# Quantised cross attention in a decoder kernel: the turning of the probabilities moved from TensorE to DMA, and their rounding from VectorE to GpSimd

## What is computed

```python
q = (x @ Wq + bq).reshape(1, B * N, H, hd)            # H = 16 heads of hd = 16
kv = (cond @ Wkv + bkv).reshape(1, -1, 2, H, hd)
k, v = (kv[:, :, 0], kv[:, :, 1])
q = jnp.transpose(q * scale, (0, 2, 1, 3))            # k and v likewise, without the scale
q = _fq_sym(q, axis=-1); k = _fq_sym(k, axis=-1); v = _fq_sym(v, axis=2)
attn = jnp.einsum('bhqd,bhkd->bhqk', q, k)
attn = jax.nn.softmax(attn.astype(jnp.float32), axis=-1)
attn = _fq_unsigned(attn, axis=-1)                    # s = max/255; round(attn/s), 0 to 255, times s
out = jnp.einsum('bhqk,bhkd->bhqd', attn, v)
```

## Time and profile before

| what | value |
|---|---|
| median of three runs | 2290.28 us |
| the profiled execution's own time | 2290.69 us |
| its span | 2288.9 us |
| TensorE busy | 1893.1 us, 83% |
| VectorE busy | 1271.6 us, 56% |
| ScalarE busy | 806.8 us, 35% |
| GpSimd busy | 253.6 us, 11% |
| first score product to last row written, attention block | 1034.72 to 1331.25 us |

### The profile page before, as it was taken

One profiled execution on the slowest core, in us unless ns is written; L12 is line 12 of the kernel. 1 busy time (PEld: TensorE's weight loads), 2 busy tenths in 40 slices (PEclk: granted clock), 3 DMA queues, 4 the chain that ended last, 5 costly groups with the idle time before them and its releaser, 6 DMA issues. The chain is left out here.

```text
span 2288.9 us, 25404 instructions
## 1 busy us (share of the span) xinstructions
PE 1893.1 (83%) x8989; PEld 1106.2 (48%) x8990; DVE 1271.6 (56%) x2123; ACT 806.8 (35%) x1349; POOL 253.6 (11%) x256
## 2 busy tenths in 40 slices
PE   6899599844646666748999979989977999999998
PEld 4566246532312222435555553355645565555555
DVE  3457522467459999679999954434643222222224
ACT  2257211135354333127888832215621111111111
POOL 0100202021003322320000011110050000000000
PEclk9999799977778889875555579997997999999999
DMA  1100000110000000100000000000001323223220
GB/s 73 60 1 2 19 0 22 48 42 1 26 0 1 0 0 0 56 11 1 1 1 1 2 28 0 0 0 1 2 11 55 111 82 95 87 89 89 87 80 19
DMA packets 25002, 68.93 MB, mean 30 GB/s; under 512 B 3456, under 2 KB 10880, under 8 KB 23488
## 3 DMA queue, kind: packets, MB, share of 16 engines
q1 hardware_dynamic: 24896, 67.55, 9.3%
HBM read 66.23 MB, written 1.31 MB: 30 GB/s over the span
## 5 line engine op out<-in xcount | busy, mean ns | idle before, releaser
L2317 PE MATMUL psum<-XT,l3f_wgu 128*128 128x512 f32 x768 | 337.4, 592 | 0.0
L2359 DVE TENSOR_TENSOR l3f_h<-l3f_silu,psum 128x512 f32<-128x512 f32 x96 | 66.0, 688 | 363.1 <-ACT l3f_silu L2343 363.1
L2317 PEld LDWEIGHTS psum<-XT,l3f_wgu 128*128 128x128 f32 x768 | 145.9, 190 | 163.8 <-issue 161.3
L1581 PE MATMUL psum<-l_drive,consts 128*128 128x512 f32 x256 | 148.5, 710 | 92.3 <-DVE l_drive L1679 92.3
L2343 ACT ACTIVATE l3f_silu<-psum 128x512 f32<-128x512 f32 x96 | 57.3, 597 | 430.6 <-PE psum L2317 430.6
L2308 PE MATMUL psum<-l3f_wd,l3f_h 128*128 128x256 f32 x784 | 177.0, 379 | 0.0
L1903 ACT ACTIVATE l2x_rings<-psum,l2x_mx,l2x_q_s 128x1024 f32<-128x1024 f32 x128 | 154.2, 1205 | 47.1 <-DVE l2x_mx L1861 45.8
L2308 PEld LDWEIGHTS psum<-l3f_wd,l3f_h 128*128 128x128 f32 x784 | 149.0, 190 | 40.7 <-issue 23.0
L424 POOL TENSOR_TENSOR rstd<-var,minus_half 128x1 f32<-128x1 f32 x104 | 66.2, 637 | 914.0 <-DVE var L395 914.0
L1859 DVE TENSOR_REDUCE l2x_mx<-psum 128x1 f32<-128x1024 f32 x128 | 156.0, 1218 | 9.8 <-PE psum L1826 8.1
L1836 PEld LDWEIGHTS psum<-l2x_id,l2x_rings 128*128 128x128 f16 x1024 | 98.8, 141 | 126.0 <-DVE l2x_rings L1869 126.0
(11 more groups left out here) (439 smaller groups left out, 3099.9 us busy)
## 6 DMA issues: line engine op xcount, KB each, us to landing
l3f_wgu<-in_expert_gu SPq DMA_DIRECT2D x48, 256.0 KB, 2.6
l3f_c_all<-token_weights SPq DMA_DIRECT2D x32, 384.0 KB, 4.2
l3f_c_all<-token_weights SPq DMA_DIRECT2D x32, 256.0 KB, 4.3
l3f_wd<-in_expert_down SPq DMA_DIRECT2D x48, 128.0 KB, 2.4
l3f_c_all<-token_weights SPq DMA_DIRECT2D x32, 128.0 KB, 4.2
arena<-in_pack SPq DMA_DIRECT2D x1, 3660.0 KB, 11.9
arena<-in_pack SPq DMA_DIRECT2D x1, 3277.0 KB, 10.4
arena<-in_pack SPq DMA_DIRECT2D x1, 2688.0 KB, 9.9
```

Source lines behind the costliest of these rows:

```text
L1581: last = nc.tensor.matmul(k.bank(4 + 2 * e + half), k.identity[:, :], drive[:, (2 * i + e) % 4, half * HALF:(half + 1) * HALF], start=n == ...
L2317: last = nc.tensor.matmul(k.bank(2 * half + n), wgu[:, slot, c, n * P:(n + 1) * P], k.XT[:, c, half * HALF:(half + 1) * HALF], start=c == ...
```

## The change

- The scores have three pairs of banks (0 to 5), so that unit i waits for the exponential of unit i - 3. TensorE's transposes, their float16 identity and the copies out of PSUM are gone.
- The bias of the exponential has ln 255 added, in the instruction that scales the maximum. So the exponential and its sum are 255 times as large, the multiplication in the rounding and the 1/255 at the end of a tile fall away.
- GpSimd rounds: one instruction on 128 x 1024 float32 adds 1.5 * 2^23 and takes it away again, and writes bfloat16 into the ring `whole` of 3.
- SyncE issues for each unit one DMA with transpose=True, from `whole` into `pT`, now a ring of 4 with a semaphore for each slot. 256 KB a unit.
- The values come five units behind the scores in place of four.

```diff
-        rings = k.sb(ctx, "l2x_rings", [P, 6 * T])
+        rings = k.sb(ctx, "l2x_rings", [P, 13 * T // 2])
-        e16 = rings[:, 3 * T:9 * T // 2].bitcast(F16).rearrange("p (n t) -> p n t", n=3)
-        pT = rings[:, 9 * T // 2:].bitcast(BF16).rearrange("p (n c t) -> p n c t", n=3, c=TILES)
+        whole = rings[:, 3 * T:9 * T // 2].bitcast(BF16).rearrange("p (n t) -> p n t", n=3)
+        pT = rings[:, 9 * T // 2:13 * T // 2].bitcast(BF16).rearrange("p (n c t) -> p n c t", n=4, c=TILES)
...
-                nc.vector.tensor_copy(f16_id[:, :], k.identity[:, :])
...
+        units, lag = TILES * heads, 5
+        turned_into = [k.sem(f"l2x_turned_into{slot_}") for slot_ in range(4)]
+        score_banks = lambda u: k.psum[:, 2 * (u % 3):2 * (u % 3) + 2, :]
             @block.tensor
-                        if i >= 2:
-                            pe.wait_ge(exp, i - 1)
+                        if i >= 3:
+                            pe.wait_ge(exp, i - 2)
...
-                    if 2 <= i < units + 2:
-                        u = i - 2
-                        pe.wait_ge(rounded, u + 1)
...
-                            last = nc.tensor.transpose(k.bank(4 + u % 2).bitcast(F16)[:, c * P:(c + 1) * P],
-                                                       e16[:, u % 3, c * P:(c + 1) * P], f16_id[:, :])
-                    if i >= 4:
-                        u = i - 4
+                    if i >= lag:
+                        u = i - lag
+                        pe.wait_ge(turned_into[u % 4], 16 * (u // 4 + 1))
...
             @block.vector
-                        k.link(dve, "dve_step", nc.vector.tensor_reduce(
-                            mx[:, i % 4, 0:1], k.psum[:, 2 * (i % 2):2 * (i % 2) + 2, :], AX.XY, ALU.max, negate=True))
-                        nc.vector.tensor_scalar(mx[:, i % 4, 1:2], mx[:, i % 4, 0:1], q_s[:, i:i + 1], None,
-                                                ALU.mult).then_inc(max_, 1)
+                        nc.vector.tensor_reduce(mx[:, i % 4, 0:1], score_banks(i), AX.XY, ALU.max,
+                                                negate=True).then_inc(max_taken, 1)
...
+                        dve.wait_ge(max_taken, i + 1)
+                        nc.vector.tensor_scalar(mx[:, i % 4, 1:2], mx[:, i % 4, 0:1], q_s[:, i:i + 1], LOG_255,
+                                                ALU.mult, ALU.add).then_inc(bias_ready, 1)
-                        nc.vector.tensor_scalar(e16[:, u % 3, :], e[:, u % 3, :], 255.0, 1024.0,
-                                                ALU.mult, ALU.add).then_inc(rounded, 1)
...
-                        nc.vector.tensor_scalar(pT[:, u % 3, :, :], k.bank(4 + u % 2).bitcast(F16)
...
-                        k.link(dve, "dve_step", nc.vector.tensor_scalar(k.recip[:, :], k.recip[:, :], 1.0 / 255, None,
-                                                                        ALU.mult))
...
             @block.scalar
+                    act.wait_ge(bias_ready, i + 1)
+                    if i >= 3:
+                        act.wait_ge(rounded, i - 2)
...
-                        nc.scalar.activation(pT[:, u % 3, :, :], k.bank(4 + u % 2).bitcast(F16)
-                                             .rearrange("p (c t) -> p c t", c=TILES), ACT.Copy,
-                                             bias=-1024.0).then_inc(by_act, 1)
+            @block.gpsimd
+            def _(pool):
+                for i in range(units):
+                    pool.wait_ge(exp, i + 1)
+                    if i >= 3:
+                        pool.wait_ge(turned_into[(i - 3) % 4], 16 * ((i - 3) // 4 + 1))
+                    nc.gpsimd.tensor_scalar(whole[:, i % 3, :], e[:, i % 3, :], ROUND, -ROUND,
+                                            ALU.add, ALU.add).then_inc(rounded, 1)
+            @block.sync
+            def _(sp):
+                for i in range(units):
+                    sp.wait_ge(rounded, i + 1)
+                    if i >= 4:
+                        sp.wait_ge(added, i - 3)
+                    sp.dma_start(pT[:, i % 4, :, :], whole[:, i % 3, :], transpose=True).then_inc(turned_into[i % 4], 16)
```

More of the change, by code:

```diff
@@ L8 @@
 from contextlib import ExitStack
+import math
 import numpy as np
@@ L30 @@
 ROUND = 1.5 * 2.0 ** 23
+LOG_255 = math.log(255.0)
 STAGES = range(0, 12)
@@ L1716, in l2_xattn @@
     bq, bk, bv, bp = (w(n) for n in ("bq", "bk", "bv", "bp"))
-    F16 = mybir.dt.float16
     with ExitStack() as ctx:
@@ L1808, in l2_xattn @@
         project(k, "l2x_turn_kv", heads // 2 + 2, turn_kv, turn_kv_out)
[L1811 to L1815, removed]
+        units, lag = TILES * heads, 5
+        names = ("scores", "max_taken", "bias_ready", "exp", "rounded", "added", "row")
+        scores, max_taken, bias_ready, exp, rounded, added, row_done = (k.sem("l2x_" + n) for n in names)
+        turned_into = [k.sem(f"l2x_turned_into{slot_}") for slot_ in range(4)]
+        score_banks = lambda u: k.psum[:, 2 * (u % 3):2 * (u % 3) + 2, :]
         with nc.Block("l2x_attention") as block:
@@ L1818, in _ @@
             def _(pe):
-                for i in range(units + 4):
+                for i in range(units + lag):
                     if i < units:
@@ L1822, in _ @@
                         rows = slice(h % 2 * slot, h % 2 * slot + 3 * hd)
-                        if i >= 2:
-                            pe.wait_ge(exp, i - 1)
+                        if i >= 3:
+                            pe.wait_ge(exp, i - 2)
                         for half in range(HALVES):
-                            last = nc.tensor.matmul(k.bank(2 * (i % 2) + half), qT[rows, h // 2, tile * P:(tile + 1) * P],
+                            last = nc.tensor.matmul(score_banks(i)[:, half, :], qT[rows, h // 2, tile * P:(tile + 1) * P],
                                                     kT[rows, h // 2, half * HALF:(half + 1) * HALF],
@@ L1846, in _ @@
                         for c in range(TILES):
-                            last = nc.tensor.matmul(k.bank(6 + tile % 2)[:, h * hd:(h + 1) * hd], pT[:, u % 3, c, :],
+                            last = nc.tensor.matmul(k.bank(6 + tile % 2)[:, h * hd:(h + 1) * hd], pT[:, u % 4, c, :],
                                                     v[:, c, h * hd:(h + 1) * hd], start=c == 0, stop=c == TILES - 1)
@@ L1852, in _ @@
             def _(dve):
[L1853 removed]
+                for i in range(units + lag):
                     if i < units:
[L1855 removed]
                         dve.wait_ge(scores, i + 1)
+                        nc.vector.tensor_reduce(mx[:, i % 4, 0:1], score_banks(i), AX.XY, ALU.max,
+                                                negate=True).then_inc(max_taken, 1)
                         if i >= 4:
                             dve.wait_ge(exp, i - 3)
[L1859 to L1880 removed]
+                        dve.wait_ge(max_taken, i + 1)
+                        nc.vector.tensor_scalar(mx[:, i % 4, 1:2], mx[:, i % 4, 0:1], q_s[:, i:i + 1], LOG_255,
+                                                ALU.mult, ALU.add).then_inc(bias_ready, 1)
+                    if i >= lag and (i - lag + 1) % heads == 0:
+                        tile = (i - lag) // heads
                         dve.wait_ge(added, heads * (tile + 1))
@@ new lines, in _ @@
+                for i in range(units):
+                    tile, h = divmod(i, heads)
+                    act.wait_ge(bias_ready, i + 1)
+                    if i >= 3:
+                        act.wait_ge(rounded, i - 2)
+                    if h == 0 and tile >= 2:
+                        act.wait_ge(row_done, tile - 1)
+                    nc.scalar.activation(e[:, i % 3, :], score_banks(i).rearrange("p b t -> p (b t)"),
+                                         ACT.Exp, bias=mx[:, i % 4, 1:2], scale=q_s[:, i:i + 1],
+                                         accum_out=sums[:, tile % 2, h:h + 1]).then_inc(exp, 1)
```

7 lines of the change are left out of this document (1 added, 6 removed).

## The result

The changed kernel took 2464.30 us (median of four runs, 2462.37 to 2464.84), the kernel before 2291.63 (four runs): a ratio of 1.0758, interval 1.0741 to 1.0775. It is slower by 7.6%. The profiled execution took 2464.38 us, its span was 2462.6, 173.7 over the span before.

What follows compares the result with a forecast made beforehand. Three engines with little slack, VectorE and TensorE 94% busy, bound the attention block; GpSimd's rounding would become last. 3.46 + 127 x 2.46 + 2.50, plus landing, values and end, gave 322.6 us against 296.5: 2316 in all, range 2185 to 2375.

Steps and rivals of the forecast that it cites:

- the slow tail: Whole time over 2375 us, by a transfer that is last or a rounding near 3.4 us (+142); chance 0.10.
- What the change takes away: Attention block: without transposes, copies and VectorE's rounding, a unit would take about 1.45 us; adding ln 255 costs nothing.
- GpSimd's rounding: Attention block, one instruction a unit on 128 x 1024, float32 to bfloat16: 2.50 us.
- a second estimate, 2.20: GpSimd's ns a column, from tensor-scalar rows of 256 columns (852 ns) and 2 columns (294 ns).
- The bounds: GpSimd's rounding lies between 1.22 us (twice a 512-column CAST) and 3.41 us (four times the 852 ns row).
- The Trainium skill's rule: By it GpSimd's rounding would take about as long as VectorE's maximum, as in the faster rival (2193 us, chance 0.26).
- Start to start 2.46: Back to back, GpSimd's roundings in the attention block start 2.46 us apart, each slightly before the other's end.
- The DMA: Turning 256 KB a unit takes about 1 us of the queue and 3.0 us to landing; the rings don't bind.
- My bad case: Turning DMA cuts a unit into 1024 pieces of 256 B at 137 ns each: 8.8 us a unit.
- The sum: Attention block with GpSimd last: 322.6 us against 296.5, so +26.1, less the identity cast's 0.23: +25.9.
- What would show it: Signs of being right: GpSimd over 95% busy, roundings near 2500 ns without idle time, exponentials waiting for them, block about 323 us.
- Behind the block: Blocks after the attention block may start at another clock; costed at nothing, within 2 us either way.

## Why the prediction was wrong

The direction and the mechanism held: GpSimd is last, and everything stands behind it. The size did not, and the time lies outside the range: 2464 us against 2316 forecast and 2375 at most. Even the slow tail with its rounding near 3.4 us, 142 us more than before, ends at 2432. Step by step:

- **What the change takes away** held nearly, and is hidden. VectorE's small product lasts 0.21 us as before, so the addition of ln 255 costs nothing there, but it starts 1255.81 - 1254.48 = 1.33 us after the maximum's start, where it was 1.26; why was not separated. With the rounding on VectorE the next instruction starts 1151.93 - 1150.48 = 1.45 us after the maximum's start, not 1.39. Without any rounding a unit takes 1.64, not 1.45; there the DMA engines are busy 92%, which I had not put into that sentence.
- **GpSimd's rounding** is the step that failed: 2.50 us forecast, 3.63 measured. It has two errors. The slope of 2.15 ns a column was that of tensor against tensor, and a second estimate, 2.20, seemed to confirm it. But that one used an instruction on 2 columns for the fixed part: 294 ns, where the rows of 256 to 1024 columns leave 0.2 us fixed. With the true 2.50 ns a column one addition takes 2.77 us, 0.27 more. The second addition I took to be free: I called the row "of the same operation", but its instruction does one operation, a multiplication (line 1104 of the kernel before), and the change's does two. The second costs 0.83 ns a column, 0.86 us. Together 0.27 + 0.86 = 1.13.
- **The bounds** failed by the same neglect. The upper one, 3.41, scaled the 852 ns row by columns and left the number of operations as it was in that row.
- **The Trainium skill's rule**, that one-input operations of GpSimd are roughly at line rate ("GPSIMD Engine Reference", section 4.1), holds for the copy alone, 1039 ns against VectorE's maximum of 1217. For tensor-scalars the trace disagrees, with 2771 and 3628 ns; the same rounding took VectorE 683.
- **Start to start 2.46** from 2.50: the shape held, 3.59 from 3.63.
- **The DMA** held: 3.1 us to landing where 3.0 was taken, 1.46 us of the queue where about 1 was, between the ends of 0.83 and 8.8. My bad case had the size of the pieces about right, 256 B, and their price wrong: 1.46/64 = 23 ns of an engine in place of 137. The two pages of the Trainium skill that the prediction named can be compared too. "VectorE: DVE Perf Modes", section "The three transpose paths", gives 1309 ns for one square of 128 by 128: for the pace, eight squares do not take eight times that, but 1.46 us. "Advanced Engine Details and Errata", section "X-Bar Transpose (TRN2)", calls turning DMAs as fast as others: here 256 KB took 1.46 us of the sixteen engines, against 0.83 by the rate of the large load. That load comes from HBM; no plain transfer within SBUF was run beside it.
- **The sum** is right with the measured terms: 3.52 + 127 x 3.594 + 3.63 + 3.12 + 0.42 + 0.71 = 467.8 us, measured 467.8.
- **What would show it** came in its kind: GpSimd at 100%, no idle time between its instructions, the exponential released by the rounding. Its sizes went with the rounding: 3628 ns where 2500 stood, a block of 467.8 us for 323, VectorE at 41% and TensorE at 37% where 60% was written.
- **Behind the block** the time is 2.7 us longer, where I had allowed 2 for the clock. TensorE's products are busy 2.5 us more there (894.72 against 892.20), at a mean granted clock of 0.95 both times; what caused it is open.

## What to carry to other kernels

An instruction that moves to another engine is priced by its own form: the number of its operations as well as its columns, from a row with the same number, or else with a term for each. A fixed part is taken from two sizes of working length, not from an instruction on two columns. And before a loop's work goes to a fourth engine, compare its instruction with the pace of the loop: here 3.63 us against 2.32 took more than three relieved engines gave, while sharing the work with ScalarE, and one operation less, gave 2.4%.

## What the runs showed of the hardware that was not expected

- GpSimd's tensor-scalar on float32 costs 2.50 ns a column for one addition and 0.83 for the second, whether it writes float32 or bfloat16; its copy to bfloat16 costs 0.83.
- VectorE's float32-to-bfloat16 rounding between SBUF buffers and GpSimd's rounding disturb each other: 683 ns becomes 1.2 us, or 3628 becomes 4057 ns, or both, while the maximum out of PSUM keeps its 1.22 us. One that starts 0.14 to 0.88 us ahead of GpSimd's end ends 0.54 to 0.55 us past it (54 of 64 roundings).
- DMA turns 256 KB (128 x 1024 bfloat16) in 1.46 us of sixteen engines and 3.1 us to landing; landings stay at 3.3 in the median at a DMA share of 0.92.
